# Ternary weight preparation between expert tiles: four transposes to a bank, and five steps a tile from expert 6 on

## What is computed

```python
def _ternary(w):                                   # W1 [4096,1024], W2 [1024,4096]
    scale = jnp.maximum(jnp.mean(jnp.abs(w)), 1e-08)
    return jnp.clip(jnp.round(w / scale), -1.0, 1.0)
h = gelu(jnp.einsum('bsd,fd->bsf', x, _ternary(W1)) + b1)
out = jnp.einsum('bsf,df->bsd', h, _ternary(W2)) + b2
```

```python
h1 = jnp.maximum(jnp.einsum('th,ehf->etf', xt, W1) + b1[:, None, :], 0.0)
ye = jnp.einsum('etf,efh->eth', h1, W2) + b2[:, None, :]
```

## Time and profile before

| | |
|---|---|
| runs | median 8269.31 us of 5 (8260.5 to 9070.96) |
| the profiled execution | 8272.4 us |
| its slowest core, core 2 | span 8270.9 us (the eight: 8223.1 to 8270.9 us) |
| TensorE, matmuls | 6159.6 us busy, 74% of the span |
| VectorE | 2524.2 us, 31% |
| ScalarE | 1739.2 us, 21% |
| the chain that ended last | TensorE 65%, VectorE 11%, DMA 10%, ScalarE 6% |
| transposes L853 and L886 | 256 each |

### The profile page before, as it was taken

The page is one execution under the profiler, slowest core; times in us unless marked ns, Lnnn a source line. Parts: engine busy times, 40 slices in busy tenths (PEclk is TensorE's granted clock), DMA queues, the critical chain, the costliest instruction groups (busy, mean ns, idle before and its releaser), DMA issues.

```text
span 8270.9 us, 73554 instructions; the slowest of 8 cores (8223.1 to 8270.9 us)
## 1 busy us (share of the span) xinstructions
PE 6159.6 (74%) x25424; PEld 2496.4 (30%) x25424; DVE 2524.2 (31%) x5029; ACT 1739.2 (21%) x2768; POOL 152.5 (2%) x177
## 2 busy tenths in 40 slices
PE   3344699999997888788887878835565666676687
PEld 1111244444443333333333333312211121222233
DVE  4645322222223223222222222365443323223000
ACT  1000111111111111111111111100033646475121
POOL 0000000000000000000000000000000000000000
PEclk9555699999998898899898989958876777777898
DMA  1000232233233212211212121011112020200423
GB/s 50 4 0 0 46 62 49 44 62 76 53 71 56 44 36 48 59 31 32 53 28 56 29 53 32 17 60 39 21 35 31 1 31 1 31 1 13 119 74 80
DMA packets 164150, 336.81 MB, mean 41 GB/s; under 512 B 12131, under 2 KB 53900, under 8 KB 161364
## 3 DMA queue, kind: packets, MB, share of 16 engines
q0 software_dynamic: 107888, 221.31, 15.3%
q1 hardware_dynamic: 55908, 110.79, 4.1%
HBM read 445.96 MB, written 46.14 MB: 59 GB/s over the span
## 4 chain that ended last, share of the span: by engine, by line
PE 65%; DVE 11%; DMA 10%; ACT 6%; issue 6%; DVEq 2%; POOL 0%; ACTq 0%; SPq 0%; POOLq 0%
PE pA L701 21%; PE pB L717 11%; PE pC L717 11%; ACT expT L1079 4%; PE pA L1198 3%; DMA denM<-den_stg 2%; DMA w2t_sc<-buf 2%; PE pB L1212 1%; DMA w1t_sc<-buf 1%; PE pC L1212 1%; PE pA L931 1%; PE pC L1101 1%; PE pD L616 1%; DVE recS L586 1%; DVE buf L772 1%
## 5 line engine op out<-in xcount | busy, mean ns | idle before, releaser
L701 PE MATMUL pA<-xnT,W1q 128*128 128x512 bf16 x8192 | 1829.9, 385 | 0.3 <-DMA W2q<-L_W 0.3
L706 ACT ACTIVATE h<-pA,b1c 128x512 bf16<-128x512 f32 x1024 | 703.8, 687 | 3682.2 <-PE pA L701 3682.2
L701 PEld LDWEIGHTS pA<-xnT,W1q 128*128 128x128 bf16 x8192 | 810.0, 99 | 992.7 <-issue 59.2
L731 DVE SCALAR_TENSOR_TENSOR acc<-pB,G,acc 128x512 f32<-128x512 f32 x512 | 383.7, 751 | 2292.4 <-PE pB L717 1681.9
L717 PE MATMUL pB<-W2q,h 128*128 128x512 bf16 x4096 | 938.2, 379 | 126.8 <-ACT h L706 120.0
L717 PE MATMUL pC<-W2q,h 128*128 128x512 bf16 x4096 | 937.6, 379 | 0.0
L717 PEld LDWEIGHTS pB<-W2q,h 128*128 128x128 bf16 x4096 | 383.8, 98 | 640.6 <-issue 211.2
L1079 ACT ACTIVATE expT<-pA,shcol 128x512 bf16<-128x512 f32 (+1 forms) x704 | 465.4, 744 | 414.9 <-PE pA L1070 358.6
L731 DVE SCALAR_TENSOR_TENSOR acc<-pC,G,acc 128x512 f32<-128x512 f32 x512 | 384.1, 751 | 542.7 <-PE pC L717 350.3
L717 PEld LDWEIGHTS pC<-W2q,h 128*128 128x128 bf16 x4096 | 390.3, 98 | 482.1 <-issue 29.0
L1086 DVE TENSOR_TENSOR expT<-expT,s_masks 128x512 bf16<-128x512 bf16 (+1 forms) x640 | 270.4, 425 | 811.0 <-ACT expT L1079 789.7
(11 more groups left out here) (254 smaller groups left out, 3891.4 us busy)
## 6 DMA issues: line engine op xcount, KB each, us to landing
W1q<-L_W POOLq DMA_DIRECT2D x32, 2048.0 KB, 18.3
W2q<-L_W POOLq DMA_DIRECT2D x32, 2048.0 KB, 30.5
wbuf<-L_W SPq DMA_DIRECT2D x32, 1024.0 KB, 12.1
w2tb<-w2t_sc POOLq DMA_DIRECT2D x8, 4096.0 KB, 17.2
wbuf<-L_W SPq DMA_DIRECT2D x32, 512.0 KB, 10.4
wbuf<-L_W SPq DMA_DIRECT2D x64, 256.0 KB, 3.9
WOb<-L_WO POOLq DMA_DIRECT2D x8, 2048.0 KB, 15.7
o<-stg POOLq DMA_DIRECT2D x64, 256.0 KB, 3.9
```

The source lines that it names most:

```text
L701: t_p1 = mm.mark(TE.raw.matmul(PS[bk], lhsT=W1q[:, s, a, ft * 128:(ft + 1) * 128], rhs=xnT[:, a, tq * 512:(tq + 1) * 512], start=(a == 0), ...
L706: bank_free[bk] = sc.mark(SE.raw.activation(h1[:, ft, :], PS[bk], ACT.Relu, bias=b1c0[:, e, qq * 8 + ft:qq * 8 + ft + 1]))
L731: bank_free[bk] = vv.mark(VE.raw.scalar_tensor_tensor(out=aslc, in0=PS[bk], scalar=G[:, tq * 4 + ts_, e:e + 1], in1=aslc, op0=OP.mult, op1 ...
```

## The change

The helper `ternarize` is replaced by `tern_group4`, which puts four transposes into one bank and then ternarizes the four together: one wait for the last transpose, a drain, four is_lt, a drain, four combining operations, one release of the bank. A W1 step is four such groups that alternate between banks 6 and 7, a W2 unit is one group, and successive units alternate between the banks. The wait for the last store, `t_st`, is made by TensorE ahead of the group's transposes, not by VectorE. From expert 6 on (the 25th tile) five steps are taken after a tile, not two.

```diff
-                                for _ in range(2):
+                                for _ in range(2 if e < 6 else 5):
                                     if next(tern_gen, "END") == "END":
...
-                def ternarize(ps_ap, dst_ap, thc, deps):
-                    VE.wait(t_thrc, *deps)
-                    sl_ = tern_ctr[0] % 4
-                    if sl_ == 0:
-                        VE.raw.drain()
-                    tern_ctr[0] += 1
-                    VE.raw.tensor_scalar(out=ttmp[:, sl_, :], in0=ps_ap,
-                                         scalar1=thrc[:, thc + 1:thc + 2],
-                                         scalar2=None, op0=OP.is_lt)
+                def tern_group4(bk, srcs, dsts, thc, deps):
+                    use_bank(bk)
+                    TE.wait(tk["consts"], *deps)
+                    for i4, s_ap in enumerate(srcs):
+                        tr = mm.mark(TE.raw.transpose(
+                            PS[bk][:, i4 * 128:(i4 + 1) * 128], s_ap, ident32[:]))
+                    VE.wait(tr, t_thrc)
                     VE.raw.drain()
-                    return vv.mark(VE.raw.scalar_tensor_tensor(
-                        out=dst_ap, in0=ps_ap, scalar=thrc[:, thc:thc + 1],
-                        in1=ttmp[:, sl_, :], op0=OP.is_gt, op1=OP.subtract))
+                    for i4 in range(4):
+                        VE.raw.tensor_scalar(out=ttmp[:, i4, :],
+                                             in0=PS[bk][:, i4 * 128:(i4 + 1) * 128],
+                                             scalar1=thrc[:, thc + 1:thc + 2],
+                                             scalar2=None, op0=OP.is_lt)
+                    VE.raw.drain()
+                    for i4 in range(4):
+                        tt_ = vv.mark(VE.raw.scalar_tensor_tensor(
+                            out=dsts[i4], in0=PS[bk][:, i4 * 128:(i4 + 1) * 128],
+                            scalar=thrc[:, thc:thc + 1],
+                            in1=ttmp[:, i4, :], op0=OP.is_gt, op1=OP.subtract))
+                    bank_free[bk] = tt_
+                    return tt_
...
-                    for ftl in range(2):
-                        for a2_ in range(DT):
-                            bk = 6 + (ftl * 8 + a2_) % 2
...
+                    for g4 in range(4):
+                        ftl, a0 = g4 // 2, (g4 % 2) * 4
+                        srcs = [wbuf[:, s, ftl * 1024 + (a0 + j) * 128:
+                                     ftl * 1024 + (a0 + j + 1) * 128] for j in range(4)]
+                        dsts = [buf1[:, a0 + j, ftl * 128:(ftl + 1) * 128]
+                                for j in range(4)]
+                        tt_ = tern_group4(6 + g4 % 2, srcs, dsts, 0, (t_l[s], t_st))
...
+                    srcs = [wbuf[:, s, fl * 128:(fl + 1) * 128] for fl in range(4)]
+                    dsts = [buf2[:, fl, dc2 * 128:(dc2 + 1) * 128] for fl in range(4)]
+                    tt_ = tern_group4(6 + u % 2, srcs, dsts, 2, (t_l[s], t_st))
```

## The result

The changed kernel takes 0.9949 times the time of the kernel before (95% interval 0.9931 to 0.9967), and 0.9938 (0.9909 to 0.9967) in a second set of runs: 42 and 51 us faster, where 64 were forecast. In many executions of every kernel here the cores of one die ran at a lower clock and took longer; times and ratios of executions in this document leave these out, so the median over the first six runs, 8526.58 us, says nothing of the change. The others of these six lie at 8215.5 to 8227.6 us, inside the range of 8188 to 8234, and 10 to 23 us above the predicted 8205. The profiled execution took 8225.0 us, against 8272.4 before and a forecast of 8208.4; its slowest core is core 5.

The account below looks back on a forecast made before the run. TensorE bounds the expert feed-forward, its matmuls stopping for ternary steps (about 655 us). Gains 27.3+4.5+4.2+9.3+14.7+4 = 64.0 us take the profiled 8272.4 to 8208.4, or 8205 at the runs' median; range 8188 to 8234.

Parts of the forecast that it names:

- the one on the W1 stops: W1 stops: w1t_sc store lands with the weights, whose end stays put; each double stop 3.9 us shorter, 27.3 for seven.
- The 2 us saved ahead of the store: W1 stops: work before the store falls from 13.2 to 11.2 us; counted at nothing, at most 16 us over eight stops.
- After the landing: W1 stops: TensorE leaves 7.2 us after the store lands, against 11.1 before; single stop from 11.65 to 7.2.
- the rival on VectorE: Groups of four: the eight operations don't overlap, 0.48 us more per waited group, 26 us; gain 38, time 8231; chance 0.08.
- that on both bounds: Groups of four: operations don't overlap and transposes run in series; nothing left, 8269 us, no change; chance 0.05.
- W2 stops: Three W2 stops before expert 6: TensorE leaves at 21.3 us against 24.4, 3.1 each, 9.3 gained.
- Experts 6 and 7: Stops and end there: five long stops of 48.0 or 47.3 us, 238.6 against 253.3, 14.7 gained.
- The returns: First 64 matmuls after a stop: two slow returns fewer, 2.0 us each with rounding, 4 us gained.
- the weights take longer: Thirteen stops: shifted stops make cores' weight loads meet, 7.8 us each; kernel 37 us slower, 8306; chance 0.04.
- stores land sooner too: W1 stops: stores get their turns whatever the weights do, saving 16 us; gain 80, time 8189; chance 0.14.

## Why the prediction was right in sign and short in size

- **The wait for the store.** The step that failed is the one on the W1 stops, "so I take it to wait for their end, whose time does not move". That end moved: from 26.1 to 28.4 us on the first core of a pair and from 28.3 to 33.0 on the later one. On the later cores the store does not wait for it either, but lands 3 us ahead. The landing came 1.7 us later on the mean (27.6 to 29.3), over eight stops 13.4 us: the W1 stops gained 22.6 and not 36.0, and the rest of these stops was right to within a microsecond each. What moved the landing is mainly the distance of the neighbours, which grows to 16.4 us and not to 24.8; at equal distance it moved by -0.6 to 0.3 us on the mean of the two cores. The 2 us saved ahead of the store had been priced at nothing or at a gain; with what they do to the distance they were a loss. (The Trainium skill, "DMA: Bandwidth & Descriptors", section "Queues, rings and completion order", has each DMA engine take turns between queues. The trace agrees: from 2654 to 2664 us on core 5 after the change the profile counts 673 packets of the weights' queue and 671 of the store's. The prediction drew from it a store that lands sooner; at equal distance that came on the later cores alone.)
- **The reading behind it.** The prediction saw the weight load take 31.4 us in one stop and 23.6 in another and read from it that the store waits for the weights, but not why the loads differ. Core 2 was 5.6 us behind core 3 in the first of these stops and 25.3 behind in the other.
- **After the landing**, the groups: 7.0 us for 7.2, VectorE's group 2.42 for 2.46, four transposes 1.08 for 1.09, the single stop 7.09 for 7.2. Right, and with them the rival on VectorE and that on both bounds fell.
- **W2 stops**: 21.7 us for 21.3 on the mean; before them the cores' mean was 24.3, not the 24.4 of core 2. 1.7 us of the gain are missing.
- **Experts 6 and 7**: the long stops took 48.3 us on the mean, for 48.0 and 47.3. The term was right to 3 us. But it priced two edits as one: the groups alone gain 25.8 us there (253.7 to 227.9), and the five steps take 14 of these back; without the groups they do nothing.
- **The returns**: 6.4 us for 4.
- **The rival "the weights take longer"** named the right mechanism and put it too large: its "if the shifted stops made the cores' weight loads meet" is what the later core of a pair shows, 4.7 us a stop, and its argument against ("all eight cores are shifted in the same way") fails, since the two cores of a pair stand some 8 us apart at the start, and what shifts is how fast that grows. It would decide above 4.9 us a stop; the landing moved by 1.7 on the mean. The rival "stores land sooner too" held on the later cores at equal distance, by 1.3 to 1.8 us up to 16 us apart, and nowhere else.

That the time came out inside the range is in part luck: the W1 stops were off by more than a third of their term, and the two edits of experts 6 and 7 hid each other.

Open: at equal distance the weights still end 0.4 to 2.1 us later with the store at 10.8. By the turns alone a store that starts 2.4 us sooner takes about 0.1 MB from the weights by then (34 to 41 GB/s, as below), some 0.6 us of their loading (an estimate). No run shows where the rest comes from.

## What to carry to other kernels

When a wait ends with a shared resource and not with its own work, making the work ahead of it faster can move the resource's end the wrong way: ask what the earlier issue takes turns with, and who else loads at that time. Here it was the neighbouring core, so one core's trace could not show it; compare cores, and stops at equal distance, before a mean over them is explained. The large gain here was not in the stop's operations (0.5%) but in what runs beside it: releasing prefetches behind the stall, and a second buffer for its output, gave a further 3.3% (0.9618 against 0.9949). Price each half of a change alone: one half can carry all of it and hide the other's cost.

## What the hardware showed that was not expected

Neighbouring cores share something that loads go through. With the store at 13.2 us the weights of the two end at 28.3 and 32.7 us while the cores are 4 to 8 us apart, and at 25.2 and 25.3 once they are 24 or more apart, about as long as a load takes. What a core's loads and stores move in the first double stop, before the change, in 40 slices of 1 us from 1.6 us ahead of the stop: first core 5, the first of its pair, then core 4, the later one (GB/s):

```profile
GB/s 0 0 0 20 109 213 209 203 215 211 213 217 211 211 205 193 162 162 190 139 212 211 157 143 187 183 167 181 349 408 365 123 8 0 0 0 0 0 0 0
```

```profile
GB/s 0 0 0 0 0 86 197 168 141 168 147 160 160 150 141 158 141 156 141 103 187 141 192 216 215 208 219 219 216 209 223 212 391 426 279 8 0 0 0 0
```

Both move the same 5.78 MB. The first runs at 193 to 217 for 11 us; shortly before that ends, its store is issued and its neighbour's loads begin. The later one runs at 141 to 168 for some 13 us (one slice 103), and from the 24th slice on at 208 to 223. Core 4 reaches this stop 8.0 us after core 5, so its 24th slice is core 5's 32nd, the one in which that core's traffic ends. The 16 DMA engines are shown nine tenths busy in both. (The Trainium skill, "Trainium Architecture — The Big Picture", section "The hierarchy (trn2)", has cores 0 and 1, 2 and 3, and so on share one stack of device memory; the pairs in the trace are these. That the memory is what they compete for, no run here shows.)

While the store and the weights move together, the packets of the two queues alternate one for one: 424 of the store's and 428 of the weights' on core 5 before the change from 2650 to 2656 us, 671 and 673 after it from 2654 to 2664. The store's are 512 B and the weights' 2 KB, so of the 1.71 MB that core 5 moves in the second of these stretches the store gets 0.34, 34 GB/s; on the first cores, on the mean, it gets 41 and the weights 165 GB/s instead of 210. At that pace 512 KB take 13 to 15 us; with no weights beside it the whole store lands 4.0 us after its issue.

Which core of a pair is the first changes from one profile to the next, and the slowest core of the chip is one of the later ones.
